# Weight gradients of gate and value by three float32r passes in place of one float32 matmul

## The reference, cut to what matters

```python
theta = {'gate': ttt_gate, 'val': ttt_val, 'proj': ttt_proj}   # 128x512, 128x512, 512x128

def loss_fn(p):
    h = jax.nn.swish(k_ttt @ p['gate']) * (k_ttt @ p['val'])
    pred = h @ p['proj']
    return jnp.mean((pred - v_ttt) ** 2)
for _ in range(TTT_STEPS):                                      # 2
    grads = jax.grad(loss_fn)(theta)
    theta = {kk: _muon_update(theta[kk], grads[kk]) for kk in theta}
```

## Time and profile before

| | us |
|---|---|
| median of 3 runs | 2215.02 (2212.51 to 2221.22) |
| profiled execution, its own time | 2205.43 |
| its span, first to last instruction | 2203.7 |
| PE busy over the span | 1881.1 (85%) |
| DVE busy | 1608.5 (73%) |
| ACT busy | 1242.0 (56%) |
| POOL busy | 533.0 (24%) |

### The profile page before, as it was taken

One profiled execution on the slowest core, in us unless ns is written; L12 is line 12 of the kernel. 1 busy time (PEld: TensorE's weight loads), 2 busy tenths in 40 slices (PEclk: granted clock), 3 DMA queues, 4 the chain that ended last, 5 costly groups with the idle time before them and its releaser, 6 DMA issues. The chain is left out here.

```text
span 2203.7 us, 35298 instructions
## 1 busy us (share of the span) xinstructions
PE 1881.1 (85%) x11504; PEld 1494.5 (68%) x11504; DVE 1608.5 (73%) x4124; ACT 1242.0 (56%) x2916; POOL 533.0 (24%) x606
## 2 busy tenths in 40 slices
PE   6999999999999999974873979999799987933771
PEld 4888888888888888854763437776677766623761
DVE  5999999999999999976655657775577756657333
ACT  5888888888888888863554543332233324411332
POOL 0111111111111111110656103441144401000571
PEclk9999999999999999985887789999899999855995
DMA  7000000000000000012653000000000000040444
GB/s 223 1 1 1 1 1 1 1 1 1 1 1 1 1 1 1 1 49 42 118 127 92 13 0 1 0 0 1 1 1 0 0 1 5 3 143 0 107 81 88
DMA packets 64481, 61.25 MB, mean 28 GB/s; under 512 B 10676, under 2 KB 54168, under 8 KB 64200
## 3 DMA queue, kind: packets, MB, share of 16 engines
q1 hardware_dynamic: 53944, 42.61, 6.5%
q0 software_dynamic: 10384, 16.72, 4.7%
HBM read 40.18 MB, written 18.86 MB: 27 GB/s over the span
## 5 line engine op out<-in xcount | busy, mean ns | idle before, releaser
L489 DVE TENSOR_TENSOR probT<-turn_ps,probT 128x512 fp32r<-128x512 f32 x512 | 335.1, 686 | 63.3 <-ACT probT L403 63.2
L418 ACT ACTIVATE prob<-prob,negmax 128x512 f32<-128x512 f32 x512 | 375.3, 739 | 4.5 <-DVE negmax L483 4.5
L237 POOL TENSOR_TENSOR x<-x,scaled 128x512 f32<-128x512 f32 x128 | 167.1, 1306 | 810.1 <-DVE scaled L504 810.1
L483 DVE CUSTOM_DVE_ANT_0 prob<-score_ps,bias 128x512 f32<-128x512 f32 x512 | 340.9, 684 | 6.8 <-issue 1.1
L403 ACT CAST probT<-turn_ps 128x512 fp32r<-128x512 f32 x512 | 283.7, 598 | 21.8 <-PE turn_ps L309 21.8
L309 PE MATMUL turn_ps<-ident,prob 128*128 128x128 f32 x2048 | 266.3, 273 | 1.3 <-DVE probT L489 1.1
L326 PE MATMUL work_ps<-probT,val 128*128 128x512 f32 x1024 | 257.2, 393 | 0.1
L309 PEld LDWEIGHTS turn_ps<-ident,prob 128*128 128x128 f32 x2048 | 236.7, 140 | 28.2 <-DVE probT L489 3.5
L297 PE MATMUL score_ps<-k,q 64*128 64x512 f32 x1536 | 213.0, 408 | 3.7 <-DVE negmax L483 2.3
L326 PEld LDWEIGHTS work_ps<-probT,val 128*128 128x128 f32 x1024 | 187.5, 188 | 39.8 <-DVE probT L489 1.7
L297 PEld LDWEIGHTS score_ps<-k,q 64*128 64x128 f32 x1536 | 135.0, 184 | 48.9 <-issue 19.7
(11 more groups left out here) (502 smaller groups left out, 3991.7 us busy)
## 6 DMA issues: line engine op xcount, KB each, us to landing
ew<-L_ffn_fc_weight SPq DMA_DIRECT2D x32, 256.0 KB, 3.4
bias<-bias_line SPq DMA_DIRECT2D x16, 448.0 KB, 10.7
mid_rows<-row SPq DMA_DIRECT2D x40, 128.5 KB, 4.0
last_rows<-row SPq DMA_DIRECT2D x40, 64.0 KB
rows_dram<-qk SPq DMA_DIRECT2D x1, 2304.0 KB, 18.9
acc_dram<-zero POOLq DMA_DIRECT2D x1, 2112.0 KB, 17.7
acc<-acc_dram SPq DMA_DIRECT2D x4, 528.0 KB, 6.0
x_rows<-x SPq DMA_DIRECT2D x4, 512.0 KB, 6.6
```

The lines of the kernel that those rows point to most:

```text
L237: pool.tensor_tensor(mine, mine, scaled[a][:, :, :], ALU.add).then_inc(added, 1)
L418: act.activation(mine, mine, ACT.Exp, bias=negmax[p % 2][:, i, a:a + 1], scale=-1.0, accum_out=total[p % 4][:, i, a:a + 1]).then_inc(exp_d ...
L483: dve.tensor_tensor_reduce(prob[p % 2][a][:, i, :], score_ps[i % 2][a][:, :], bias[:, h, first:first + SEQ][:, ::-1], -1.0, 3.0e38, ALU.ad ...
L489: dve.tensor_tensor(probT[1][:, g % QT, :], turn_ps[g % 2][:, :], probT[0][:, g % QT, :].bitcast(F32), ALU.subtract).then_inc(turned_lo, 1)
```

## The change

For `dwg` and `dwv` the float32 matmul is replaced by three float32r passes. This needs high and low halves of du, dv and the keys. ACT makes the three high halves, DVE makes `du_lo`, and POOL makes `dv_lo` and `ks_lo`; POOL's copy of the row of keys goes to a new buffer, `k_row`. Core of the diff:

```diff
         @block.gpsimd
-                    pool.tensor_copy(ks[p][:, :], qk[...]).then_inc(k_staged, 1)
+                    row = qk[:, bass.ds(l, 1), D:2 * D].rearrange("p a d -> p (a d)")
+                    pool.tensor_copy(k_row[p][:, :], row).then_inc(k_rows, 1)
+                o = n - 3
+                if live(o):
+                    pool.wait_ge(dv_hi, o + 1)
+                    pool.tensor_tensor(dv_parts[1 - p][1][:, :], dv[1 - p][:, :], dv_parts[1 - p][0][:, :].bitcast(F32), ALU.subtract).then_inc(dv_lo, 1)
+                if live(l):
+                    pool.wait_ge(k_hi, l + 1)
+                    pool.tensor_tensor(ks[p][1][:, :], k_row[p][:, :], ks[p][0][:, :].bitcast(F32), ALU.subtract).then_inc(k_staged, 1)
                 if live(n):
                     pool.wait_ge(slope_ready, n + 1)
...
         @block.tensor
+            def add_passes(to, left, right, o):
+                for k, (i, j) in enumerate(PASSES):
+                    mm = pe.matmul(to, left[i][:, :], right[j][:, :], start=isinstance(o, int) and o == 0 and k == 0,
+                                   stop=isinstance(o, int) and o == TILES - 1 and k == 2, skip_group_check=True)
                 return mm
...
                     pe.wait_ge(k_staged, o + 1)
-                    pe.wait_ge(du_ready, o + 1)
-                    pe.matmul(dwg_ps[:, :], ks[q][:, :], du[q][:, :], ...).then_inc(dwg_done, 1)
-                    pe.wait_ge(dv_ready, o + 1)
-                    pe.matmul(dwv_ps[:, :], ks[q][:, :], dv[q][:, :], ...).then_inc(dwv_done, 1)
+                    pe.wait_ge(du_lo, o + 1)
+                    add_passes(dwg_ps[:, :], ks[q], du_parts[q], o).then_inc(dwg_done, 1)
+                    pe.wait_ge(dv_lo, o + 1)
+                    add_passes(dwv_ps[:, :], ks[q], dv_parts[q], o).then_inc(dwv_done, 1)
...
         @block.scalar
                     act.copy(dpT[p][0][:, :], pred_ps[:, 1, :]).then_inc(dpT_hi, 1)
+                if live(o):
+                    act.wait_ge(du_ready, o + 1)
+                    if again(o):
+                        act.wait_ge(dwg_done, o - 1)
+                    act.copy(du_parts[q][0][:, :], du[q][:, :]).then_inc(du_hi, 1)
+                if live(l):
+                    act.wait_ge(k_rows, l + 1)
+                    act.copy(ks[p][0][:, :], k_row[p][:, :]).then_inc(k_hi, 1)
...
                     act.copy(vc[p][:, :], v_ps[:, :]).then_inc(v_copied, 1)
+                if live(o):
+                    act.wait_ge(dv_ready, o + 1)
+                    if again(o):
+                        act.wait_ge(dwv_done, o - 1)
+                    act.copy(dv_parts[q][0][:, :], dv[q][:, :]).then_inc(dv_hi, 1)
...
         @block.vector
+                if live(o):
+                    dve.wait_ge(du_hi, o + 1)
+                    dve.tensor_tensor(du_parts[q][1][:, :], du[q][:, :], du_parts[q][0][:, :].bitcast(F32), ALU.subtract).then_inc(du_lo, 1)
                 if live(n):
                     dve.wait_ge(sg_ready, n + 1)
...
                     if again(l):
-                        dve.wait_ge(dwv_done, l - 1)
+                        dve.wait_ge(du_lo, l - 1)
+                        dve.wait_ge(dv_lo, l - 1)
```

More of the change, by code:

```diff
@@ L1471, in ttt_grads @@
         parts = lambda name, shape: [core.sb(st, f"{name}_{half}", shape, F32R) for half in ("hi", "lo")]
-        kTs, ks = [parts(f"kTs{i}", [P, P]) for i in range(2)], sb("ks", [P, D])
+        kTs, ks = [parts(f"kTs{i}", [P, P]) for i in range(2)], [parts(f"ks{i}", [P, D]) for i in range(2)]
+        k_row = sb("k_row", [P, D])
+        du_parts, dv_parts = ([parts(f"{n}{i}", [P, HID]) for i in range(2)] for n in ("du", "dv"))
         wg, wv, wpT = (parts(n, [P, HID]) for n in ("wg", "wv", "wpT"))
@@ L1480, in ttt_grads @@
                  "h_turned", "hT_ready", "pred_done", "dp_ready", "dp_turned", "dpT_ready", "dh_done", "du_ready", "dv_ready",
-                 "dwp_done", "dwg_done", "dwv_done", "dpT_hi", "w_hi", "w_lo")
+                 "dwp_done", "dwg_done", "dwv_done", "dpT_hi", "w_hi", "w_lo", "k_rows", "k_hi", "du_hi", "du_lo", "dv_hi", "dv_lo")
         (kT_staged, k_staged, u_done, v_done, sg_ready, v_copied, s_ready, h_ready, c_ready, slope_ready, w_ready,
          h_turned, hT_ready, pred_done, dp_ready, dp_turned, dpT_ready, dh_done, du_ready, dv_ready,
-         dwp_done, dwg_done, dwv_done, dpT_hi, w_hi, w_lo) = (core.sem(n) for n in names)
+         dwp_done, dwg_done, dwv_done, dpT_hi, w_hi, w_lo, k_rows, k_hi, du_hi, du_lo, dv_hi, dv_lo) = (core.sem(n) for n in names)
         block = st.enter_context(nc.Block())
@@ L1503, in step @@
                         pool.wait_ge(dwv_done, l - 1)
-                    pool.tensor_copy(ks[p][:, :], qk[:, bass.ds(l, 1), D:2 * D].rearrange("p a d -> p (a d)")).then_inc(k_staged, 1)
+                    row = qk[:, bass.ds(l, 1), D:2 * D].rearrange("p a d -> p (a d)")
[7 more added lines that the diff above has]
+                    pool.tensor_tensor(ks[p][1][:, :], k_row[p][:, :], ks[p][0][:, :].bitcast(F32), ALU.subtract).then_inc(k_staged, 1)
                 if live(n):
@@ L1521, in three_passes @@
                     mm = pe.matmul(to, left[i][:, :], right[j][:, :], start=(k == 0), stop=(k == 2))
+                return mm
+            def add_passes(to, left, right, o):
+                for k, (i, j) in enumerate(PASSES):
+                    mm = pe.matmul(to, left[i][:, :], right[j][:, :], start=isinstance(o, int) and o == 0 and k == 0,
+                                   stop=isinstance(o, int) and o == TILES - 1 and k == 2, skip_group_check=True)
                 return mm
@@ L1561, in step @@
                     pe.wait_ge(k_staged, o + 1)
-                    pe.wait_ge(du_ready, o + 1)
-                    pe.matmul(dwg_ps[:, :], ks[q][:, :], du[q][:, :], start=isinstance(o, int) and o == 0,
-                              stop=isinstance(o, int) and o == TILES - 1, skip_group_check=True).then_inc(dwg_done, 1)
-                    pe.wait_ge(dv_ready, o + 1)
-                    pe.matmul(dwv_ps[:, :], ks[q][:, :], dv[q][:, :], start=isinstance(o, int) and o == 0,
-                              stop=isinstance(o, int) and o == TILES - 1, skip_group_check=True).then_inc(dwv_done, 1)
+                    pe.wait_ge(du_lo, o + 1)
+                    add_passes(dwg_ps[:, :], ks[q], du_parts[q], o).then_inc(dwg_done, 1)
+                    pe.wait_ge(dv_lo, o + 1)
+                    add_passes(dwv_ps[:, :], ks[q], dv_parts[q], o).then_inc(dwv_done, 1)
             run(pe, step)
@@ L1576, in step @@
                 p, q = r % 2, 1 - r % 2
-                m, l = n - 1, n - 2
+                m, l, o = n - 1, n - 2, n - 3
                 if live(l):
```

## The result

The changed kernel takes 2284.7 us (median of 4 runs, 2274.4 to 2294.9), the kernel before 2213.8 (4 runs, 2205.1 to 2221.2). The ratio is 1.031, 95% interval 1.027 to 1.036: slower by some 70 us. The forecast was slower, at 2271.

What follows compares the result with a forecast made beforehand. PE bound the kernel before; after the change, chains through DVE and POOL would set a 7.1 us step. 58 steps of +0.96 add 55.7 to 2205.4, giving 2261, plus 9.6 for the median: 2271, range 2220 to 2315.

Steps and rivals of the forecast that it cites:

- The clash: POOL's dv_lo and DVE's c, both inputs in SBUF, exclude each other; second c lengthens from 0.69 to about 1.6 us.
- The first rival: DVE takes the second c before the waiting dv_lo, so POOL is late: +90 to +108, about 2310; chance 0.17.
- The step: Steady gradient-loop step, transpose to transpose, goes from 6.14 to 7.1 us, range 6.7 to 7.4; chance 0.57.
- the forecast chain: Waits through DVE from the end of dp, over s, both c, du, dv and h to the next dp: 7.12 us.
- The chain through POOL: Waits from kTs_lo over u, sigmoid, s, c, dv_lo, ks_lo, w and kTs_hi back to kTs_lo: 7.0 us.
- The sum: 0.96 us a step over 58 steps: +55.7 us; time to compare 2271.
- charge for the clock: Nothing charged for PE's gaps in the loops: a window also 82% busy still has a granted clock of 1.00.
- PE's margin: Before the change, PE would wait for dp if over 0.20 us earlier at the transpose; caps its gain near 12 us.
- No clash: Second rival: dv_lo falls behind c or only partly blocks; step 6.0 to 6.3 us, -8 to +9; chance 0.17.
- The third rival: PE stays the bound at 5.82 us and its 18.6 us saving comes in full: 2196; chance 0.09.
- chain A: Named in the experiments: closed chain dp, transpose, u, sigmoid, s, c, c, du, dv, h, dp; 6.12 us in x3.
- Which engine shows it: Changed profile's loops: PE busy about 82%, waiting over 1 us a step for dp and kTs_lo; POOL busy 70 to 80%.

Runs made afterwards that it cites:

- x1: Changed kernel with dv_lo on POOL subtracted for 128 of 512 columns only, the rest zeroed by a memset: step 6.54 us.
- x4: Changed kernel with dv_lo moved to DVE right behind du_lo, and its cast dv_hi right behind du_hi on ACT: step 6.73 us.
- x3: Kernel before with only PE's three float32r passes of the same rounded halves per gradient, low halves left out: step 6.13 us, ratio 1.001.
- x7: Changed kernel's full arithmetic reordered: casts behind hT, dv_lo and ks_lo behind kTs, kTs ahead of w, dp ahead of h, then du_lo: 5.80 us, ratio 0.985 against kernel before.

## Why the prediction was right, and where it was not

- **The clash.** Right in place, direction and size: the second `c` 1.64 us (forecast "about 1.6"), `dv_lo` 1.38, `h` 1.00, and `dv_lo` wins the pair. The first rival, in which DVE wins, did not happen; the second `c` starts 0.04 after the first ends, and POOL is waiting by then. x1 and x4 show the cause: 0.95 of the 1.21 us is the wait of the second `c`.
- **The step.** 7.1 forecast, 7.35 measured, within the stated 6.7 to 7.4, but near its upper end. Against the forecast chain (times from the end of dp): `s` 1.94 instead of 1.80, end of the second `c` 5.04 instead of 4.90, end of `h` 7.16 instead of 6.92, of dp 7.36 instead of 7.12. So 0.14 came ahead of `s`, and 0.1 in the wait of `h` for `w` (0.32, taken as 0.2). The 0.14 is ACT's: the casts took 0.62 to 0.63 and 0.30 where 0.59 and 0.27 were taken from copies out of PSUM, `du_lo` started late by 0.06, and `s` could not follow it after 0.61, because the sigmoid behind `du_hi` and `ks_hi` ended only at 1413.10. The chain through POOL was forecast at 7.0 and closes at 7.35 as well; 0.26 of the difference is its step "kTs_hi behind `h`", 0.71 instead of 0.45, since `h` ends 0.56 after `w`, and kTs_hi after that.
- **The sum.** 58 x 0.96 = 55.7 forecast, 58 x 1.21 = 70 measured. The 14 us between 2271 and 2284.7 are this. No charge for the clock was right (1.00), and the steps that fill and drain the stages were even: 70.5 in all.
- **PE's margin.** Wrong: "The margin is thus 0.20 us". There was next to none, 0.02. The 0.20 between dp's semaphore and the transpose was used up by the 0.20 that u needs behind the transpose when PE had been waiting: with the transpose at 1407.60, u would have started at 1407.80, and it did start at 1407.82. So "the 0.20 us margin alone caps it near 12" should have been nothing at all, as x3 shows. It did not hurt the forecast, because PE was not the bound after the change.
- **The rivals.** "No clash", at 6.0 to 6.3, was not tested as such: no run takes the clash away and leaves the order as it is. x4 (6.73) puts a second subtraction ahead of `s`, and x1 (6.54) leaves a quarter of the clash at `c` and a long `h`. Taking the 0.95 at `c` and the 0.21 at `h` off the 7.35 leaves 6.2 us by estimate, and so does taking the extra 0.52 ahead of `s` off x4; the prediction's own chain through POOL came to 6.26. All three lie within the rival's band. So the rival's condition was wrong, while its price may well have been right: by this estimate the change would have cost little or nothing without the clash. The third rival, faster at 2196, could not have happened in this order: chain A is 6.12 in x3, where no work is added and 0.12 of it is `h` waiting for `w`; an estimate without that wait is 6.0, still above PE's 5.82.
- **Which engine shows it.** "PE busy in the loops about 82%": 84 and 83%. "PE waiting for dp and for kTs_lo, together over 1 us": 1.22 for dp; kTs_lo ended 0.07 ahead of u, so the wait for it was hidden behind the one for dp. "POOL busy 70 to 80% of a step" was too high: it was 63 and 64% in the two loops. The time does not hang on it.

## What to carry to other kernels

An engine that is busy 100% of a loop need not be its only bound: look for chains of waits that lead from one step back to the same instruction of the next, add up the distances from start to start, and expect a saving on the busy engine only if all of these chains are shorter than its work. Before a piece of work goes to an idle engine, ask beside which instructions it will run: here a read by POOL ahead of a DVE instruction with two SBUF inputs made DVE wait for about 1 us. The same work cost +1.21 us a step in one order and allowed -0.34 in another, so an idle stretch is worth something only at the point where the data are ready and nobody waits behind.

## What was not expected of the hardware

- After a wait of PE for dp, u starts 0.20 us behind the transpose (1411.25 to 1411.45 in the changed kernel, 1455.34 to 1455.54 in x3); when PE came late it was 0.02 to 0.03 (kernel before, x7). What makes the difference was not tried.
- In x3 PE waits for dp in every step (the transpose starts 0.06 behind it), and yet PE's busy time is 150.00 of 150 us in its loop: a pass is shown with 0.39 to 0.40 us though the next starts 0.23 behind it. So a gap of up to some 0.16 us can be hidden, and a share of 100% does not prove that PE never waited.
- An ACT cast of 512 columns from SBUF to float32r takes 0.62 us, a copy of as many from PSUM 0.59.
